# Unrolling the edge stage of a four-layer graph kernel, turning keys by bf16 products, and issuing list 1 before list 2

## The reference

```python
# 42500 edges (src, dst), sorted by dst; edge_attr_64 is 42500 x 64
x = x + gnn0(layernorm(x)); x = x + ffn0(layernorm(x)); ...   # four layers

def gnn0(x, ...):
    msg = relu(x[src] + edge_attr @ We + be)
    agg = segment_sum(msg, dst)                 # then a matmul, batch norm, relu

def ffn0(x, ...):                               # 8 experts of 3 matmuls each,
    ...                                         # summed with softmax weights

# layers 1 to 3 use the same edges again; the second MoE has a GAT router
# over its own 131072 edges, of which those with dst < 2500 matter
```

## Time and profile before

| | us |
|---|---|
| median of 3 runs (lowest to highest) | 6201.53 (6196.15 to 6212.05) |
| span of the profiled execution | 6201.5 |
| POOL busy in it | 3154.1 |
| PE busy in it | 5106.1 |
| last list 1 or list 2 add issued (start) | 3946.30 |

### The profile page before, as it was taken

One profiled execution on the slowest core, in us unless ns is written; L12 is line 12 of the kernel. 1 busy time (PEld: TensorE's weight loads), 2 busy tenths in 40 slices (PEclk: granted clock), 3 DMA queues, 4 the chain that ended last, 5 costly groups with the idle time before them and its releaser, 6 DMA issues.

```text
span 6201.5 us, 83711 instructions
## 1 busy us (share of the span) xinstructions
PE 5106.1 (82%) x25696; PEld 3214.2 (52%) x25696; DVE 3660.0 (59%) x7745; ACT 1664.6 (27%) x2761; POOL 3154.1 (51%) x2148
## 2 busy tenths in 40 slices
PE   5777777877699898989668989486765998999999
PEld 4566655655455575557556656483222333222266
DVE  7887777778511202120234521399996999777754
ACT  2221111111222201220122221126773001666521
POOL 4777888886688878786777887302220000000000
PEclk9998888787699988999887889799998999999999
DMA  7776666663444496559798866894443100232200
GB/s 182 154 152 115 122 115 123 115 92 49 44 12 15 6 123 50 16 7 115 81 186 99 88 60 62 119 213 109 111 111 82 29 27 23 81 82 81 79 14 27
DMA packets 534651, 522.74 MB, mean 84 GB/s; under 512 B 263645, under 2 KB 490002, under 8 KB 527287
## 3 DMA queue, kind: packets, MB, share of 16 engines
q1 hardware_dynamic: 271558, 427.90, 31.0%
q0 software_dynamic: 261696, 90.13, 23.0%
q10 hardware_dynamic: 1158, 1.65, 0.1%
HBM read 365.70 MB, written 153.75 MB: 84 GB/s over the span
## 4 chain that ended last, share of the span: by engine, by line
POOL 24%; PE 19%; DVE 11%; DMA 9%; issue 8%; SPq 4%; ACT 0%; DVEq 0%; ACTq 0%; POOLq 0%
POOL pairs L730 24%; DMA pairs<-PAIR_CNT,PAIR_IDX 9%; PE PS L2308 6%; PE PS L2145 5%; DVE WORK L1948 4%; DVE MXS L2186 4%; SPq L187 3%; PE PS L1001 2%; PE PS L973 2%; PE PS L2166 2%; DVE XT L534 1%; DVE WORK L1954 1%; PE PS L2296 1%; DVE ROWS L1622 1%; PE PS L2101 0%
## 5 line engine op out<-in xcount | busy, mean ns | idle before, releaser
L730 POOL DMA_INDIRECT pairs<-PAIR_CNT,PAIR_IDX x1364 | 2155.4, 1580 | 613.9 <-issue 421.6
L534 DVE SCALAR_TENSOR_TENSOR XT<-PS,ROWS,XT 128x512 f32<-128x512 f32 (+1 forms) x1364 | 937.5, 743 | 142.5 <-PE PS L526 106.4
L772 POOL DMA_INDIRECT sums<-WORK,ROWS x340 | 529.7, 1558 | 167.4 <-issue 130.2
L2379 DVE SCALAR_TENSOR_TENSOR WORK<-WORK 125x1000 f32<-125x1000 f32 x400 | 462.1, 1197 | 152.7 <-ACT WORK L2347 152.0
L1094 DVE SCALAR_TENSOR_TENSOR X<-PS,G,X 125x256 f32<-125x256 f32 x280 | 122.6, 479 | 617.7 <-PE PS L1001 579.2
L2145 PE MATMUL PS<-ROWS 32*125 32x500 f32 x3200 | 451.0, 633 | 28.9 <-DVE MXS L2186 19.3
L526 PEld LDWEIGHTS PS<-IDENT,ROWS 128*128 128x128 f32 (+1 forms) x2728 | 436.4, 229 | 56.1 <-DVEq L714 28.1
L526 PE MATMUL PS<-IDENT,ROWS 128*128 128x128 f32 (+1 forms) x2728 | 444.4, 317 | 22.6 <-DVEq L714 22.6
L2186 DVE TENSOR_REDUCE MXS<-PS 125x4 f32<-125x2000 f32 x200 | 438.8, 2235 | 22.4 <-PE PS L2166 18.4
L2347 ACT ACTIVATE WORK<-PS 125x1000 f32<-125x1000 f32 x400 | 380.0, 1002 | 239.3 <-PE PS L2296 239.3
L1936 POOL TENSOR_TENSOR WORK<-WORK,ROWS 125x500 f32<-125x500 f32 x100 | 126.0, 1260 | 596.0 <-ACT WORK L1900 596.0
(11 more groups left out here) (323 smaller groups left out, 7659.2 us busy)
## 6 DMA issues: line engine op xcount, KB each, us to landing
WORK<-pairs SPq DMA_DIRECT2D x400, 218.8 KB
pairs<-ROWS SPq DMA_DIRECT2D x75, 976.6 KB
WORK<-pairs SPq DMA_DIRECT2D x48, 1093.8 KB
WORK<-pairs SPq DMA_DIRECT2D x80, 546.9 KB
pairs<-PAIR_CNT,PAIR_IDX POOLq DMA_INDIRECT x1364
WORK<-pairs SPq DMA_DIRECT2D x40, 382.8 KB
XT<-pairs SPq DMA_DIRECT2D x12, 1093.8 KB
mask_t<-ROWS SPq DMA_DIRECT2D x40, 273.4 KB
```

The costliest lines, as they stand in the source:

```text
L534: st.go(dve.scalar_tensor_tensor(KEY_JUNK[0:n, q, 0:SUPER * n], PS[0:n, bank, 0:SUPER * n], cols[0:n, q:q + 1], weights, ALU.is_equal, ALU ...
L730: pool.indirect_dma_start(table, bass.IndirectOffsetOnAxis(idx[:, n:n + 1], 0), cnt[:, n:n + 1], None, compute_op=ALU.add).then_inc(sem(do ...
L772: pool.indirect_dma_start(sums[c], bass.IndirectOffsetOnAxis(SROW[:, k % 8:k % 8 + 1], 0), SUMMED[:, k % 8, :], None, compute_op=ALU.add). ...
L2379: dve.scalar_tensor_tensor(E3[q % 8], E3[q % 8], 1.0, A3[n % 4][0:P].unsqueeze(1).to_broadcast([P, 2, CH]), ALU.min, ALU.mult).then_inc(se ...
```

## The change

- **Unrolled.** PE, DVE, ACT and SP run the edge stage as straight code with constant waits. The bias row `L0_gnn_be` moves into the edge product (a 65th row of We and of ones), so that `x_table` is stored straight from the normed rows. The clearing memsets move from DVE to POOL, at POOL's start.
- **Rows by bf16 products.** In `setup`, PE transposes the columns once (8 transposes per 128 super-tiles). The rows are then kept in three parts whose upper halves are bf16 numbers, and one row is picked and spread over the lanes by three bf16 products of 512 columns (`key_rows`), two of 500 for the destinations of a whole group (`dst_rows`). Before, it was four fp32 products per super-tile and one per column.
- **One compare per column of edges** in place of two: one `scalar_tensor_tensor` gives both the matrix for PE and the code.
- **Coding.** Of the 256 super-tiles of list 2, 176 are coded in the edge stage (two per group, in 8 of the groups three) and 80 beside the first experts: two between the products of each of the 40 steps of `l0e`, whose loop is unrolled too. Addresses are made group by group (`coded1`, `coded2`); the wide operations and `codes_ready` go.
- **POOL's order.** From column 68 on, 132 adds of list 1 are spread over the edge stage (before: 180 from group 25 on). Then `pairs_pool` issues the remaining 208 adds of list 1 in one piece, and then all 1024 of list 2.
- **SP** clears two tables' pieces per group in the first 13 groups, then fewer.

```diff
         def edges_pool(pool):
...
-                g, j = k // GR - PG, k % GR - (GR - IN_GROUP)
-                if g == 0 and j == 0:
+                if k == FIRST1:
                     pool.wait_ge(sem("zeroed1"), 16 * (ZP + 1))
-                if g >= 0 and j >= 0:
-                    add_pair1(pool, g * IN_GROUP + j)
+                for n in range(pairs, max(0, EARLY1 * (k + 1 - FIRST1) // (K1 - FIRST1))):
+                    add_pair1(pool, n)
+                    pairs += 1
...
         def pairs_pool(pool):
 
-            pool.wait_ge(sem("codes_ready"), 1)
             pool.wait_ge(sem("zeroed2"), 16 * 2 * (ZP + 1))
-            for i in range(K2 // SUPER):
-                if IN1 + SUPER * i < K1:
-                    for n in range(IN1 + SUPER * i, IN1 + SUPER * (i + 1)):
-                        add_pair1(pool, n)
-                add_super2(pool, i)
+            for n in range(EARLY1, K1):
+                add_pair1(pool, n)
+            for n in range(K2):
+                add_pair2(pool, n)
...
+        def key_rows(pe, kind, s, bank):
+
+            rows, pick, lanes = ((KEY1_ROWS, PICK[0:S1, s:s + 1], P) if kind == 1 else
+                                 (KEY2_ROWS[s // 128], PICK[:, s % 128:s % 128 + 1], 128))
+            for part in range(3):
+                ins = pe.matmul(PS[0:lanes, bank, 0:SUPER * lanes], pick.to_broadcast([pick.shape[0], lanes]),
+                                upper(rows[:, part, :]), start=part == 0, stop=part == 2)
+            ins.then_inc(sem("key_rows"), 1)
...
                 for j in range(GR):
...
-                    dve.tensor_scalar(EQ[0:P, b, :], PS[0:P, b, 0:P], col(DSTF), None, ALU.is_equal)
-                    dve.scalar_tensor_tensor(JUNK[0:P, b, :], PS[0:P, b, 0:P], col(DSTF), TRI[0:P, 0:P],
-                                             ALU.is_equal, ALU.mult, accum_out=CODE_R[0:P, s:s + 1]
+                    k = g * GR + j
+                    if k >= 8:
+                        dve.wait_ge(sem("edge_sums"), k - 7)
+                    dve.scalar_tensor_tensor(EQ[0:P, k % 8, :], PS[0:P, g % 2, j * P:(j + 1) * P], DSTF[0:P, k:k + 1],
+                                             LOW, ALU.is_equal, ALU.mult, accum_out=CODE_R[0:P, k:k + 1]
                                              ).then_inc(sem("edge_coded"), 1)
...
                     if q + 1 < 2 * NC:
                         first(q + 1)
+                    if s == "l0e":
+                        for b in range(2):
+                            n = (i * 2 * NC + q) * 2 + b
+                            pe.wait_ge(sem("keys_coded"), SUPER * (STEPS + n - 1))
+                            key_rows(pe, 2, S2 - LATE + n, 2 + b)
                     third(q)
```

More of the change, by code:

```diff
@@ new lines, in build, with keys_of @@
+        CODE_R = flat(ROWS[:, 3, :], 1600, K1)
+        SM = flat(ROWS[:, 3, :], 1940, K1)
+        LOW = flat(ROWS[:, 4, :], 1600, P)[0:P]
+        BEFORE1 = flat(XTF, 0, 2 * SUPER - 1, P)[0:P]
+        JUNK_EARLY = flat(XTF, 1000, SUPER, SUPER * 128)
+        JUNK_LATE = flat(ROWS[:, 3, :], 0, SUPER, SUPER * 128)
+        ZP, ZL = 25, 80
+        ZERO_FIRST = 13
+        S2, LATE = K2 // SUPER, 80
+        EXTRA = S2 - LATE - 2 * (NG - 1)
+        MORE = (NG - 1) // EXTRA
+        def keys_of(g):
+            if g == 0:
+                return []
+            first = 2 * (g - 1) + min((g - 1 + MORE - 1) // MORE, EXTRA)
+            return list(range(first, first + (3 if (g - 1) % MORE == 0 and (g - 1) // MORE < EXTRA else 2)))
@@ new lines, in steps_of @@
+        def steps_of(g):
+            return [(j, 2, s) for j, s in enumerate(keys_of(g))] + [(3, 1, g)]
+        STEPS = sum(len(steps_of(g)) for g in range(NG))
+        assert keys_of(NG - 1)[-1] == S2 - LATE - 1
+        def key_rows(pe, kind, s, bank):
[5 more added lines that the diff above has]
+            ins.then_inc(sem("key_rows"), 1)
@@ L592, in edges_pe @@
             stage_end(pe)
-        def gathers(g, u):
-            return 16 if isinstance(g, int) else g * 8 + (8 if u else 16)
         N_PARAMS = 36
@@ L1011, in experts_pe @@
                         first(q + 1)
-                    third(q)
+                    if s == "l0e":
[3 more added lines that the diff above has]
+                            key_rows(pe, 2, S2 - LATE + n, 2 + b)
+                    third(q)
+            if s == "l0e":
+                for i in range(E // 2):
+                    pair_of_experts(i)
+            else:
+                with pe.Fori(0, E // 2) as i:
+                    pair_of_experts(i)
             stage_end(pe)
@@ L1096, in experts_dve @@
                                                  ).then_inc(sem(s + "_x"), 1)
+                        if s == "l0e" and j % 2:
+                            m = n * 2 + j // 2
+                            key_codes(dve, STEPS + m, 2, S2 - LATE + m, JUNK_LATE, 2 + j // 2)
+                    if s == "l0e":
+                        dve.wait_ge(sem("keys_coded"), SUPER * (STEPS + 2 * n + 2))
+                        coded2(dve, st, S2 - LATE + 2 * n, S2 - LATE + 2 * n + 2, False)
+                        st.wait()
+                        coded2(dve, st, S2 - LATE + 2 * n, S2 - LATE + 2 * n + 2, True)
+            if s == "l0e":
+                for i in range(E // 2):
+                    pair_of_experts(i)
+            else:
+                with dve.Fori(0, E // 2) as i:
+                    pair_of_experts(i)
             stage_end(dve)
```

462 lines of the change are left out of this document (221 added, 241 removed).

## The result

The changed kernel takes 6322.1 us in the median of four runs (6317.7 to 6327.0), the kernel before 6202.3 in four (6196.2 to 6212.1). The ratio is 1.0182, with a 95% interval of 1.0166 to 1.0198: slower by 1.8%. The forecast was 6205 with a range up to 6315, so the time lies above the range. The profiled execution spans 6316.9 us.

The account below looks back on a forecast made before the run. POOL's chain of adds up to `l2h` was taken as the bound: 1399 + 1231 x 1.8465 + 102 + 176.6 put its last issue at 3950.6 against 3946.30, +4 us, so 6205 us; range 6140 to 6315.

Parts of the forecast that it names:

- The frame: Whole kernel: POOL's last add landing before `l2h` plus an unchanged rest of 2250 us sets the time; everything else runs hidden.
- The edge stage: POOL's first stretch: column work, early adds and allowances sum to leaving it at 1399 us, against 1585 before.
- rival (d): Edge stage misses POOL's pace: groups keep 18.3 us in place of 16.3, +136 us, 6341 us; chance 0.10.
- DVE's 12 us a group: Edge stage: DVE needs 12 us for a group with three super-tiles, under POOL's 12.7, so POOL has the pace.
- There VectorE sets the pace: First 25 groups of the kernel before: POOL waits some 2 us per group for a sum, VectorE busy 265.57 of 316 us.
- the rest is the 2 us per group of the first 25: Edge stage: what remains of the 186 us earlier finish after 90 us of postponed adds and 60.7 us of address wait.
- List 1 in one piece: After the edge stage: 52 super-tiles each wait for the one before, 3.81 us issue to issue against 1.85, costing 102 us.
- Rival (a): List 1 lands slowly: 5.91 us issue to issue per super-tile, a term of 211 us, time 6314 us; chance 0.13.
- Rival (b): List 1's landing hides: 1.85 to 2.3 us issue to issue, term 0 to 24 us, time 6103 to 6127; chance 0.10.
- List 2: POOL's adds after list 1: ordinary landings hide behind four other adds; the old loss of 176.6 us beside table loads stays.
- rival (c): Fewer losses in list 2 as other stages run ahead: 50 to 60 of 176.6 us go, time 6150; chance 0.17.
- The other chain: All engines but POOL: `gin` 182 us earlier, `l0e` 80 us longer, ready before `l2h` near 3781, then waiting 170 us.

## Why the prediction was wrong, step by step

**The frame** was right: POOL's last landing plus a rest, the other chain hidden. SP's wait was given as about 170 us and is 237. The other chain was ready at 3818 (forecast 3781), POOL 98.5 us later than forecast.

**The edge stage** is the step that failed: "POOL leaves the edge stage at ... 1399", measured 1469.0. Column 68, from which the early adds of list 1 go, was to come at 52.65 + 68 x 3.17 + 31 = 299 us and came at 364: +65 of the +70 lie in the first 17 groups. From there on the sum held to 5 us: a group takes 16.4 us (forecast 16.3), so rival (d), a stage that keeps its old 18.3, was rightly thought unlikely, and "DVE's 12 us a group" was enough. The step allowed 21 us for the start and "for slow landings ... 10". It had no term for the clearing, though the change doubles the pieces per group in just these groups. Groups 1 to 12 alone, with 21 pieces, lost 71 us beyond their 12.7. The kernel before has groups of some 14 us for a POOL that needs 12.7, with one piece each, and I put that down to VectorE ("There VectorE sets the pace: 265.57 us busy of 316"). The run with nothing cleared refutes that reading for the new kernel: there VectorE is as busy (136.06 of 161 us, 0.845, against 0.840) and the groups take 12.7. A high busy share was not a bound. For the kernel before it stays open: no run took the clearing away from it, and in the stretch of the earlier trace rows PE waited 53.4 us for the compares of L662. For the stretch 84 to 245 us (us per group is 161 us divided by the sums' adds in it, times four):

| kernel | pieces | sums' adds | us per group | gather lands in |
|---|---|---|---|---|
| nothing cleared | 0 | 51 | 12.7 | 3.0 |
| one per group | 12 | 45 | 14.3 | 4.4 |
| before | 12 | 45 | 14.3 | |
| changed, two per group | 16 | 32 | 20.1 | 8.5 |

One piece costs 1.6 us per group, two cost 7.4. So the 25 pieces cost far more than the 31 us allowed for everything. Going back to one per group gained 31 to 35 us of the 70 at the stage's end. The others are the 1.6 to 1.9 us for each piece at a slower rate in groups without early adds, which I had hoped to shed: "the rest is the 2 us per group of the first 25" was counted as gone and for the most part is not.

**List 1 in one piece** was right in mechanism and in size: 102 forecast, 117.7 measured, and the two-way test (taken away in the new kernel -119 us, put into the kernel before +98 us) shows it. The row of 3.81 us was close to the median of 3.75; what was under-sized is the tail, which one row can't show. Rival (a), 5.91 from issue to issue for all, did not happen. Rival (b) did not either. The figure of the Trainium skill, DMA: Bandwidth & Descriptors (Anatomy of one DMA), 2.0 us of fixed cost, was laid out wrongly by me: I added to it only the gap of 0.30. Measured, POOL stands 2.20 us after the 1.54 us of its own instruction, so a fixed cost of 2.0 us that begins when the instruction ends is close, and an estimate by the page in that reading is 1.54 + 2.0 = 3.5 us where the trace has 3.75.

**List 2** lost 189.5, not 176.6. The losses sit in the same stages of the other chain as before (before and now, from one stage's end to the next: `l2a` with the stage after it 43 and 41, `l2m` 43 and 46, the shifts after it 38 and 37), though all of these now come 80 us earlier: that speaks against rival (c), fewer losses for a chain that is ahead. The nine kernels with the unrolled edges lost 182 to 194 and the two with the old ones 176 and 179, so part of the 13 us is likely real. The clearest difference is in `l1g`, 26 against 15. It has 24 to 29 in all nine edited kernels, but the old kernel with the new order is one of them (29) and loses only 179 in all, so one trace per kernel does not settle where the 13 us come from. No run took the table loads away. That they cause the losses rests on where these stand, not on an experiment.

**The other chain.** `gin` starts 116 us earlier, not 182, mostly because of the edge stage. `l0e` is longer by 51 us from its first product to its last (408.3, now 459.6), and by 57 us from the end of the stage before it to its own end; forecast 80, in bounds of 50 to 110. The term was over-sized since a bf16 product takes little more than half of the fp32 row used for it: the 220 that the trace has are busy 56.7 us, 0.26 each, against 0.44. PE is busy 464.11 us of the stage against 410.47. That `l1g` no longer waits for list 1 was right.

**After the last issue** the span holds 2267.8 us, in the kernel before 2255.2. Over the nine edited kernels, the one built on the kernel before among them, it lay between 2258 and 2268 whatever was edited, so most of these 13 us is what executions differ by.

**The chances.** The time is 6322, near rival (a)'s 6314, but by another mechanism: (a) gave 109 us to slow landings in list 1, which took 16, and most of the rest came from a place that no rival named. Rival (d) had the right stage, but asked for a POOL that waits for ACT or PE in the 68 later groups; what came were waits for DMA in the first 17. A rival "two pieces per group hold up the landings" could have been given a first price from the kernel before, by taking the 1.6 us that its groups with one piece need beyond POOL's 12.7 for the clearing's; what two cost, no row of that kernel shows.

## What to carry to other kernels

When a change bunches bulk writes into a stretch, price them by what they do to the small transfers that the bounding queue waits for, even if the queue that issues them is idle; a price measured at one per period says nothing on two. A wait for the landing of one's own last write costs that landing each time (here 1.9 us), and one or two issues of independent work in between remove it, so two lists to separate tables are better interleaved than put one behind the other. An engine that is 84% busy while another waits is not shown to set the pace: look at what the one that waits is waiting for.

## What the runs showed of the hardware

- Landings of GpSimd's gathers beside bulk writes of 977 KB to HBM do not grow evenly: 3.0 us with none, 3.9 and 4.4 in two kernels with one per 14 us, 8.5 with two per 20 us. The Trainium skill, DMA: Bandwidth & Descriptors (Queues, rings and completion order), has each DMA engine take turns between its queues packet by packet. The direction agrees, and no run here shows the turns themselves.
- The same piece costs 1.6 to 1.9 us where POOL has only columns' work, and next to nothing where adds to other tables stand in between (0.9 pieces per group of 17.0 us: 6.2 us of waits in 830). In the changed kernel groups 17 to 24, with 15 early adds and 6 pieces, lose 0.4 us in all; the same groups with 8 pieces and no early add lose 15 and 17. The rate counts too: 1.1 pieces per group, with more adds beside them, brought 23.3 us of waits in 800.
- An add of 128 values of 4 bytes to scattered rows in HBM lands 2.2 us after POOL's instruction of 1.54 us ends, in nine of ten cases under 2.7, and in the worst of 52 about 8 us.
